# Eight heads' maxima of layer 1 moved among the next element's first scores, value and Gram tiles placed anew

## The chip, the cores and the metric

The kernel runs on one core of a Trainium2 chip. The core has a matrix engine (TensorE, PE in the profile), three engines for elementwise work and reductions (VectorE, DVE; ScalarE, ACT; GpSimd, POOL), and SyncE (SP), which here issues all DMAs. The engines run their own instruction queues in order and meet through semaphores. The metric is the time of one execution on the device in microseconds (us).

## The reference

Two layers of cross attention over 32 elements (B = 32) with 112 queries of 320 channels, 375 context tokens of 512 channels, and 20 heads of 16. Layer 0 attends to 77 text tokens and to the other 298 tokens with separate softmaxes and adds the two. Layer 1 attends to 371 tokens, forms from the same probabilities a mean context vector per head, and lets its cosine with four image tokens add to their scores:

```python
# layer 0
q = heads(x @ Wq.T)
k, v = heads(text @ Wk.T), heads(text @ Wv.T)            # text = ctx[:, :77]
k_ip, v_ip = heads(ip @ Wk_ip.T), heads(ip @ Wv_ip.T)    # ip = ctx[:, 77:]
out = merge(attend(q, k, v)) + merge(attend(q, k_ip, v_ip))
x = out @ Wo.T + bo + x
# layer 1
scores_t = einsum('bhsd,bhtd->bhst', q, k_t) * attn_scale # text = ctx[:, :-4]
probs_t = softmax(scores_t)
text_out = einsum('bhst,bhtd->bhsd', probs_t, v_t)
qsem = l2norm(einsum('bhst,bte->bhse', probs_t, text))
fused = einsum('bhsd,bhnd->bhsn', q, k_ip) * attn_scale + 0.5 * qsem @ l2norm(ip).T
ip_out = (softmax(fused) * side) @ v_ip
x = (text_out + ip_out) @ W_out + b_out + x
```

## The kernel before

All weights stay on the chip. `stage_order` writes out one list of stages (L57 on), and each engine's function walks this same list and does its own part of each stage. So the order of the list is the order of each engine's queue. `o.share(buffer, slots, ...)` notes who may overwrite a buffer when: the next user of a slot waits until the last reader of the one before has signalled.

PSUM has ST (three banks), PN (two banks, PV and NS) and three single banks R. ST and PN have one slot each.

An element b goes through these parts:

- **Keys, queries, values, Gram tiles** (`ahead`): matmuls on the context, split in high and low halves so that three products give full precision. A key tile (`k`) has 12 matmuls, then ScalarE copies the high part, VectorE subtracts it (`rem`) and, in every other tile, casts the middle part; GpSimd makes the low part, SyncE writes all to HBM, from where `k_stack` and `q_stack` load them as Ks and Qs. A value tile (`v_mm`, `v`) and a Gram tile (`g`) have 12 matmuls and are copied by ScalarE, Gram tiles also by VectorE. `split` makes high and low halves of the context of element b + 2: four copies on ScalarE, four subtractions on GpSimd. It needs the last Gram tile of element b.
- **Maxima** (`s_max`): scores of two or three heads with queries in the partitions, 375 columns a head. A step of three heads ("wide") goes to ST, one of two to PN. VectorE reads the maxima to m0 or m1, in layer 1 also the four image scores to `sip`. When all 20 heads are read, `m_T` transposes the maxima on TensorE, ScalarE copies them, GpSimd splits them in three (`m_split`, `mrem` and `ms`), and SyncE writes them as extra rows of Qs, by six DMAs in layer 0 and three in layer 1. The scores need these rows.
- **Scores, exponentials, products with values** (`scores`, `pv0_set`, `pv1`, `y`): groups of four heads, keys in the partitions. Scores go to ST; ScalarE takes the exponential out of ST.
- **Finish** (`pvT`, `o_T`, `o_mm`, `x1_T`, and `ns_T`, `fuse`, `ip_softmax`, `ip_T`, `ip_mm` in layer 1): transposes, output projection and the image part.

The parts of three elements overlap. The order of the list around the change, in one turn of the loop over b: scores of layer 0 of element b with key tiles and queries of b + 1 in between; scores of layer 1 of b - 1; maxima of layer 0 of b + 1, then maxima of layer 1 of b. Among the 16 maxima steps `between` (L413 on) places the finish of b - 1 (`last`), and after steps 2, 4, 6, 8, 11, 12, 14 and 16 one value or Gram tile (`pieces`): layer 1 values 0 to 2 and Gram tiles 0 to 2 of b in turn, at last values 1 and 2 of layer 0 of b + 1. The last of them stands between the last maxima step and the first scores. Right behind the first scores comes `m_T` of layer 1.

Of the kernel before, what the change touches and what calls it, by code (L numbers as in the profile page):

```python
# [1 line left out]

# [13 lines left out]
PV_SETS = ((0, 1, 2), (3, 4))  # L16
SETS_FROM = 2
EPS2 = 1e-24
QROWS = [(0, 3), (3 * D, 2), (5 * D, 1)]
# [11 lines left out]
class Order:  # L31
# [3 lines left out]
    def __init__(self):  # L35
        self.stages, self.nth, self.many = [], {}, {}
        self.ring, self.slot, self.freed = {}, {}, {}

    def add(self, kind, *key):
# [4 lines left out]
    def at(self, kind, *key):  # L44
        return self.nth[kind, key]
# [15 lines left out]
def stage_order():  # L61
# [87 lines left out]

    def maxima(b, l, between):  # L150
        for h in range(0, H, 5):
            for h0, wide in ((h, True), (h + 3, False)):
                o.add("s_max", b, l, h0, wide)
                if wide:
                    o.share("ST", 1, ("s_max", b, l, h0), "s_max_read", o.at("s_max", b, l, h0, wide))
                else:
                    for part in ("PV", "NS"):
                        o.share(part, 1, ("s_max", b, l, h0), "s_max_read", o.at("s_max", b, l, h0, wide))
                between()
        return m_rows(b, l)  # L160

    def m_rows(b, l):
        yield
        o.add("m_T", b, l)
        in_bank(("m_T", b, l), "m_hi", o.at("m_T", b, l))
        yield
        o.add("m_split", b, l)
# [84 lines left out]
    def finish1(b):  # L252
# [22 lines left out]
        o.add("out", b)  # L275

    def take(pieces, n):
        for _ in range(n):
            next(pieces, None)
# [56 lines left out]

    rows0 = maxima(0, 0, among)
    flush()
# [5 lines left out]
    for b in range(B + 1):  # L344
# [3 lines left out]
        first, last = iter(()), iter(())  # L348

        def among0(g):  # L350
            take(rows1, 1)
            if not b and g == 2:
                o.add("k_stack", 1, 0, 0)
            if not b and g == 3:
                o.add("ctx", 2)
            take(pieces, 1 if b + 1 < B and (b or g < 4) else 0)
            if g < 2:
                flush()
# [54 lines left out]
        def between():  # L413
            count[0] += 1
            if count[0] > 9:
                take(rows0, 1)
            if count[0] in (1, 2, 3, 5, 7, 9, 10):
                take(last, 1)
            if count[0] in (2, 4, 6, 8, 11, 12, 14, 16):
                take(pieces, 1)  # L420
            if not b and count[0] > 9:
                warm("R", (4, 0, 2, 3, 2, 3, 3)[count[0] - 10])
            if b + 1 == B:
                warm("R", 2)
        if b + 1 < B:
            rows0 = maxima(b + 1, 0, between)
            take(rows0, 1)
        if b + 1 == B:
            take(pieces, 4)
        if b < B:  # L430
            rows1 = maxima(b, 1, between)
            take(rows1, 1)
# [34 lines left out]
def xattn_two_layers(nc, a, out):  # L467
# [3 lines left out]
    with ctx:  # L471
# [198 lines left out]
        def tensor(e):  # L670
            w = Waiter(e)
            for kind, key in o.stages:
# [119 lines left out]
                elif kind == "s_max":  # L792
                    b, l, h0, wide = key
                    n, to = (3, ST) if wide else (2, PN)
                    w.wait_ge(d_kr[l][0 if h0 + n <= HALVES[0][1] else 1], 96 * (b + 1))
# [11 lines left out]
                elif kind == "m_T":  # L807
                    b, l = key
                    n = 2 * H if l == 0 else H
                    free(w, "R", ("m_T", b, l))  # L810
                    w.wait_ge(s_max_read, 8 * at("m_T", b, l))
                    e.transpose(R[slot["R", ("m_T", b, l)]][0:n, 0:S], (m0, m1)[l][:], ident[0:S, 0:S]).then_inc(m_T, 1)
# [161 lines left out]
        def vector(e):  # L974
# [8 lines left out]
            for kind, key in o.stages:  # L983
# [77 lines left out]
                elif kind == "s_max":  # L1061
                    b, l, h0, wide = key
                    n, to = (3, ST) if wide else (2, PN)
                    w.wait_ge(s_max_mm, at("s_max", *key))
# [619 lines left out]
```

## Time and profile before

| | us |
|---|---|
| median of 3 runs | 2555.74 |
| lowest and highest | 2554.03, 2556.6 |
| span of the profiled execution | 2557.0 |
| TensorE busy (matmuls) | 2466.0 (96%) |
| VectorE busy | 1634.3 (64%) |
| ScalarE busy | 1226.5 (48%) |
| GpSimd busy | 768.3 (30%) |
| mean granted clock of TensorE | 0.994 |

The profiled execution is one more run. Its span is 1.3 us above the median of the others. Busy time of TensorE counts matmuls from start to end, and they overlap, so a wait shows best as the distance from one start to the next. Behind a row of the timeline, "[0.56 <-DVE m L1069]" means that the engine stood idle for 0.56 us until that instruction of VectorE had ended.

### The profile page before, as it was taken

To read this page: it belongs to the slowest core of one execution; us is meant where nothing else is said; L and a number is where in the kernel's file an instruction comes from. 1 tells how busy PE (TensorE), PEld (TensorE's weight loads), DVE (VectorE), ACT (ScalarE), POOL (GpSimd) and SP (SyncE) were. 2 spreads that over 40 slices of the span, in tenths; PEclk is the share of its full clock that TensorE was granted. 3 is DMA by queue.
4 is the path that set the end of the run, shared out by engine and by line. 5 is a ranking of instruction groups with operands and counts; after the bars stand their busy time and mean duration, and the time that the engine had idled before them with its cause. 6 is when DMAs were issued, how large, how long until landed. Compare 5 with 4: busy or idle time off the path is not lost.

```text
span 2557.0 us, 64247 instructions
## 1 busy us (share of the span) xinstructions
PE 2466.0 (96%) x26500; PEld 2147.6 (84%) x26500; DVE 1634.3 (64%) x3217; ACT 1226.5 (48%) x2251; POOL 768.3 (30%) x998
## 2 busy tenths in 40 slices
PE   7899999999999999999999999999999999999998
PEld 7788888888888888888888888888888888888877
DVE  4365667656667666677655677656676656676655
ACT  3355444455444555444554444554444554444543
POOL 3123233232233332333232232332332332332322
PEclk9999999999999999999999999999999999999999
DMA  8765556664456755467655466645566644566620
GB/s 213 135 104 81 93 88 96 104 107 79 88 87 99 117 84 88 85 94 111 103 82 87 84 107 100 109 75 89 97 93 105 93 84 88 88 97 102 94 28 18
DMA packets 373418, 241.47 MB, mean 94 GB/s; under 512 B 133675, under 2 KB 366971, under 8 KB 373116
## 3 DMA queue, kind: packets, MB, share of 16 engines
q1 hardware_dynamic: 373126, 237.36, 56.6%
q8 instruction: 210, 3.44, 0.7%
q14 instruction: 82, 0.67, 0.1%
HBM read 171.35 MB, written 64.59 MB: 92 GB/s over the span
## 4 chain that ended last, share of the span: by engine, by line
PE 76%; DVE 17%; SPq 2%; DMA 2%; issue 2%; ACT 1%; POOL 0%; DVEq 0%; POOLq 0%; ACTq 0%
PE ST L821 7%; DVE w L981 5%; PE R L887 5%; PE PN L860 5%; PE R L763 5%; PE R L708 4%; PE R L776 4%; PE R L777 4%; DVE m L1069 4%; PE R L709 4%; PE PN L905 3%; PE R L945 3%; PE R L779 3%; PE R L711 3%; DVE w L978 2%; PE R L890 2%
## 5 line engine op out<-in xcount | busy, mean ns | idle before, releaser
L1445 POOL TENSOR_TENSOR w<-w 128x448 f32<-128x448 f32 (+1 forms) x256 | 330.8, 1292 | 381.2 <-DVE w L978 362.9
L981 DVE SCALAR_TENSOR_TENSOR w<-p,pr 128x1344 f32<-128x1344 f32 x160 | 296.7, 1854 | 164.1 <-ACT pr L1331 151.5
L1303 ACT ACTIVATE p<-ST 128x1344 f32<-128x1344 f32 x260 | 335.5, 1290 | 102.0 <-PE ST L824 97.0
L887 PE MATMUL R<-pr,Gh 128*128 128x448 f32 (+1 forms) x960 | 366.1, 381 | 0.0
L978 DVE TENSOR_TENSOR rem<-R,kst 128x298 f32<-128x298 f32 (+2 forms) x180 | 89.5, 497 | 425.4 <-ACT kst L1186 425.4
L978 DVE TENSOR_TENSOR w<-R,w 128x448 f32<-128x448 f32 (+1 forms) x480 | 281.7, 620 | 68.5 <-PE R L892 57.8
L1379 POOL TENSOR_TENSOR kst<-rem,kst 128x298 bf16<-128x298 f32 (+2 forms) x180 | 147.9, 822 | 531.5 <-ACT kst L1186 290.9
L776 PE MATMUL R<-wvh,ch 128*128 128x320 f32 (+3 forms) x896 | 302.2, 337 | 0.0
L777 PE MATMUL R<-wvh,cl 128*128 128x320 f32 (+3 forms) x896 | 276.7, 309 | 0.0
L821 PE MATMUL ST<-Qs,Ks 100*128 100x112 bf16 (+1 forms) x3520 | 229.3, 214 | 8.6 <-ACT p L1303 3.5
L821 PEld LDWEIGHTS ST<-Qs,Ks 100*128 100x128 bf16 (+1 forms) x3520 | 188.1, 98 | 47.2 <-issue 14.3
L708 PE MATMUL R<-ch,wkh 128*128 128x298 f32 (+1 forms) x636 | 215.2, 338 | 2.1 <-POOL cl L1379 2.1
L1186 ACT ACTIVATE pvt<-PN 128x112 f32<-128x112 f32 (+2 forms) x260 | 88.7, 341 | 247.7 <-PE PN L909 192.3
L779 PE MATMUL R<-wvl,ch 128*128 128x320 f32 (+3 forms) x672 | 207.4, 309 | 0.0
L1331 ACT ACTIVATE pr<-ST 128x1344 fp32r<-128x1344 f32 x160 | 205.1, 1282 | 0.0
L709 PE MATMUL R<-cl,wkh 128*128 128x298 f32 (+1 forms) x636 | 199.8, 314 | 0.0
L887 PEld LDWEIGHTS R<-pr,Gh 128*128 128x128 f32 (+1 forms) x960 | 175.7, 183 | 22.6 <-issue 6.2
L1073 DVE TENSOR_REDUCE m<-ST 112x3 f32<-112x1113 f32 x128 | 168.0, 1312 | 13.1 <-PE ST L805 13.1
L890 PE MATMUL R<-pr,Gl 128*115 128x448 f32 (+1 forms) x480 | 176.3, 367 | 0.0
L892 PE MATMUL R<-pr,Gl 128*128 128x448 f32 (+1 forms) x480 | 175.6, 366 | 0.0
L1186 ACT ACTIVATE V<-R 128x320 f32<-128x320 f32 (+3 forms) x161 | 67.9, 436 | 211.4 <-PE R L780 211.4
L776 PEld LDWEIGHTS R<-wvh,ch 128*128 128x128 f32 (+3 forms) x896 | 161.0, 180 | 8.0 <-issue 0.5
(221 smaller groups left out, 5956.7 us busy)
## 6 DMA issues: line engine op xcount, KB each, us to landing
Ks<-k_split SPq DMA_DIRECT2D x384, 140.6 KB, 5.8
Ks<-k_split SPq DMA_DIRECT2D x384, 93.8 KB, 7.8
w<-in_ctxT SPq DMA_DIRECT2D x31, 750.0 KB, 9.7
k_split<-kst SPq DMA_DIRECT2D x64, 281.2 KB, 3.6
k_split<-kst SPq DMA_DIRECT2D x64, 223.5 KB, 2.8
Qs<-q_split SPq DMA_DIRECT2D x64, 210.0 KB, 8.2
q_split<-qst SPq DMA_DIRECT2D x128, 84.0 KB, 2.4
Qs<-q_split SPq DMA_DIRECT2D x64, 140.0 KB, 8.4
```

The source lines that it names most:

```text
L708: e.matmul(r[:, 0:t1 - t0], wh[:, k, c0:c0 + 128], h[:, k, t0:t1], start=k == 0, stop=False)
L709: e.matmul(r[:, 0:t1 - t0], wh[:, k, c0:c0 + 128], lo[:, k, t0:t1], start=False, stop=False)
L776: e.matmul(r[0:n, 0:C], h[:, k, :], wh[:, k, :], start=k == 0, stop=False)
L777: e.matmul(r[0:n, 0:C], lo[:, k, :], wh[:, k, :], start=False, stop=False)
L779: e.matmul(r[0:n, 0:C], h[:, k, :], wl[:, k, :], start=False, stop=False)
L821: e.matmul(ST[:, u, S * h:S * h + S], Ks[l][0:m, GH * g + h, 128 * u:128 * u + 128], Qs[l][0:m, GH * g + h, :], start=True, stop=True)
L887: e.matmul(r[0:nj, 0:QW], Gh[0:ROWS[u], q:q + nj], x[0:ROWS[u], QW * u:QW * u + QW], start=u == 0, stop=False)
L890: e.matmul(r[0:nj, 0:QW], Gl[0:ROWS[u], q:q + nj], x[0:ROWS[u], QW * u:QW * u + QW], start=False, stop=False)
L978: return e.tensor_tensor(to, x, y, op)
L981: return e.scalar_tensor_tensor(out=to, in0=x, scalar=s, in1=y, op0=op0, op1=op1)
L1303: e.activation(to.rearrange("p (u q) -> p u q", u=3), st, ACT.Exp).then_inc(p_whole, 1)
L1445: e.tensor_tensor(first, first, w2[n % 2][0:ROWS[j], QW * j:QW * j + QW], ALU.add).then_inc(ns_added, 1)
```

## The change

Elements for which `defers(b)` holds (b = 1 to 30) do only the first 12 heads of layer 1's maxima in their old place: steps of 3, 2, 3, 2 and 2 heads. The other eight heads follow in four steps of two, all in PN, after the first scores of layer 0 of the next element, after its first key tile, after its second scores and after its queries. `m_T` of layer 1 moves from behind the first scores to behind the third, `m_split` behind the first products with values. Among the maxima that stay, the value and Gram tiles come after steps 1, 2, 4, 5, 7, 8, 10 and 12, so that the last step of two heads (in ST) stands right in front of the first scores. `split` moves with the last Gram tile.

```diff
+ALL_STEPS = [(h + d, n, d == 0) for h in range(0, H, 5) for d, n in ((0, 3), (3, 2))]
+NOW_STEPS = [(0, 3, True), (3, 2, False), (5, 3, True), (8, 2, False), (10, 2, True)]
+LATE_STEPS = [(h, 2, False) for h in range(12, H, 2)]
...
-    def maxima(b, l, between):
-        for h in range(0, H, 5):
-            for h0, wide in ((h, True), (h + 3, False)):
-                o.add("s_max", b, l, h0, wide)
...
+    def max_step(b, l, h0, n, wide):
+        key = (b, l, h0, n, wide)
+        o.add("s_max", *key)
+        for part in ("ST",) if wide else ("PV", "NS"):
+            o.share(part, 1, ("s_max", b, l, h0), "s_max_read", o.at("s_max", *key))
+
+    def maxima(b, l, steps, between):
+        for step in steps:
+            max_step(b, l, *step)
+            between()
         return m_rows(b, l)
...
+    def defers(b):
+
+        return SETS_FROM <= b + 1 < B
...
+        late = iter(LATE_STEPS if b and b < B and defers(b - 1) else ())
+
+        def late_step():
+            for step in islice(late, 1):
+                max_step(b - 1, 1, *step)
+
         def among0(g):
-            take(rows1, 1)
+            if b < B and defers(b - 1):
+                late_step()
+                take(rows1, 1 if g > 1 else 0)
+            else:
+                take(rows1, 1)
...
             take(pieces, 1 if b + 1 < B and (b or g < 4) else 0)
+            late_step()
...
-            if count[0] in (2, 4, 6, 8, 11, 12, 14, 16):
+            if count[0] in ((1, 2, 4, 5, 7, 8, 10, 12) if defers(b) else (2, 4, 6, 8, 11, 12, 14, 16)):
                 take(pieces, 1)
...
-            rows1 = maxima(b, 1, between)
+            rows1 = maxima(b, 1, NOW_STEPS if defers(b) else ALL_STEPS, between)
...
-                    w.wait_ge(s_max_read, 8 * at("m_T", b, l))
+                    w.wait_ge(s_max_read, o.max_steps[b, l])
```

VectorE, from the last maxima steps of layer 1 of element 9 to the queries of element 11. Before (L1073 and L1074 read a maxima step, `rem0` is the key tile's remainder, `qrem` and `qst` are the queries'):

```order
L1073 TENSOR_REDUCE m1<-ST 112x3
L1074 COPY sip1<-ST 112x12
L1073 TENSOR_REDUCE m1<-PN 112x2
L1074 COPY sip1<-PN 112x8
L978 TENSOR_TENSOR rem0<-R1,kst0 128x298
L981 SCALAR_TENSOR_TENSOR qrem<-R2,qst 128x336
L1060 CAST qst<-qrem 128x3x112
```

Now (L1094 and L1095 read a maxima step):

```order
L1094 TENSOR_REDUCE m1<-ST 112x2
L1095 COPY sip1<-ST 112x8
L1094 TENSOR_REDUCE m1<-PN 112x2
L1095 COPY sip1<-PN 112x8
L999 TENSOR_TENSOR rem0<-R0,kst0 128x298
L1094 TENSOR_REDUCE m1<-PN 112x2
L1095 COPY sip1<-PN 112x8
L1094 TENSOR_REDUCE m1<-PN 112x2
L1095 COPY sip1<-PN 112x8
L1002 SCALAR_TENSOR_TENSOR qrem<-R1,qst 128x336
L1081 CAST qst<-qrem 128x3x112
L1094 TENSOR_REDUCE m1<-PN 112x2
```

The reads of heads 14 to 17 stand behind the key tile's remainder, and that of heads 18 and 19 behind the cast of the queries.

ScalarE, from the last Gram tile of element 10 (`Gh`, `g4`) to the maxima of layer 0 of element 11 (`mrem`, `ms`); `ch0` is the split, `x1T` the transposed o of element 9, `V1` a value tile. Before:

```order
L1186 ACTIVATE Gh<-R1 128x115
L1186 ACTIVATE g4<-R1 128x4
L1186 ACTIVATE x1T<-R2 128x2x112
L1186 ACTIVATE x1T<-R2 64x112
L1186 ACTIVATE mrem<-R0 40x112
L1186 ACTIVATE ms<-R0 40x112
L1186 ACTIVATE V1<-R2 115x20x16
L1186 ACTIVATE Gh<-R0 115x115
L1186 ACTIVATE g4<-R0 115x4
L1186 ACTIVATE ch0<-w2 128x375 x4
```

Now:

```order
L1207 ACTIVATE Gh<-R0 115x115
L1207 ACTIVATE g4<-R0 115x4
L1207 ACTIVATE ch0<-w2 128x375 x4
L1207 ACTIVATE x1T<-R1 128x2x112
L1207 ACTIVATE x1T<-R1 64x112
L1207 ACTIVATE mrem<-R2 40x112
L1207 ACTIVATE ms<-R2 40x112
```

The last Gram tile and the split have moved ahead of x1T and of the maxima's copies.

GpSimd at the same place (`cl0` is the split's low half). Before:

```order
L1450 TENSOR_TENSOR vbd<-vbd,bmask_sb 80x320
L1379 TENSOR_TENSOR mrem<-mrem,ms 40x112
L1434 CAST ms<-mrem 40x112
L1379 TENSOR_TENSOR ms<-mrem,ms 40x112
L1379 TENSOR_TENSOR cl0<-w2,ch0 128x375 x4
L1386 TENSOR_TENSOR g4<-g4,ninv 128x12
```

Now:

```order
L1471 TENSOR_TENSOR vbd<-vbd,bmask_sb 80x320
L1400 TENSOR_TENSOR cl0<-w2,ch0 128x375 x4
L1407 TENSOR_TENSOR g4<-g4,ninv 128x12
L1400 TENSOR_TENSOR mrem<-mrem,ms 40x112
L1455 CAST ms<-mrem 40x112
L1400 TENSOR_TENSOR ms<-mrem,ms 40x112
```

The split of the layer 0 maxima, which stood ahead of the context's low half, stands behind it.

## Rows read from the trace of the kernel before

**Rows 1.** The page, part 1: busy us (share of the span) and instructions of each engine.

```profile
PE 2466.0 (96%) x26500; PEld 2147.6 (84%) x26500; DVE 1634.3 (64%) x3217; ACT 1226.5 (48%) x2251; POOL 768.3 (30%) x998
```

**Rows 2.** Stretches: us, busy us (instructions) by engine, PEclk, DMA share, GB/s.

```profile
880.68:893.38 12.70, 11.71 (x74) 9.97 (x74) 12.03 (x33) 4.95 (x11) 0.79 (x1) 1.00 0.75 158
893.38:905.87 12.49, 12.23 (x80) 10.56 (x78) 10.66 (x20) 4.17 (x16) 4.78 (x8) 1.00 0.11 29
905.87:911.66 5.79, 5.79 (x69) 5.52 (x68) 0.84 (x4) 4.71 (x9) 1.58 (x4) 1.00 0.02 3
```

**Rows 3.** Timeline of TensorE, the maxima of one element: start us, us, engine, line, what.

```profile
888.51 0.37 PE L803 MATMUL PN<-Ks,Qs 96*112 96x375 bf16 x1 [0.56 <-DVE m L1069]
...
897.01 0.44 PE L776 MATMUL R<-wvh,ch 128*115 128x320 f32 x1
...
898.90 0.32 PE L803 MATMUL PN<-Ks,Qs 96*112 96x375 bf16 x1
...
899.09 0.41 PE L788 MATMUL R<-ch 128*115 128x256 f32 x1
...
900.65 0.48 PE L803 MATMUL ST<-Ks,Qs 96*112 96x375 bf16 x2
```

**Rows 4.** Timeline of VectorE, the same stretch.

```profile
881.36 0.40 DVE L1068 TENSOR_REDUCE m<-ST 112x3 f32<-112x231 f32 x1
...
882.67 0.17 DVE L978 TENSOR_TENSOR zq<-zs 112x20 f32<-112x20 f32 x1
...
883.04 0.31 DVE L1068 TENSOR_REDUCE m<-PN 112x2 f32<-112x154 f32 x1
...
883.95 0.27 DVE L1155 RECIPROCAL sm<-d 112x20 f32<-112x20 f32 x1
...
899.42 0.93 DVE L1073 TENSOR_REDUCE m<-PN 112x2 f32<-112x742 f32 x1 [0.69 <-PE PN L805]
900.27 0.15 DVE L1074 COPY sip<-PN 112x8 f32<-112x8 f32 x1
```

**Rows 5.** Timeline of ScalarE, the same stretch.

```profile
894.34 0.50 ACT L1186 ACTIVATE x1T<-R 128x224 f32<-128x224 f32 x2 [0.27 <-PE R L937]
...
901.06 1.73 ACT L1186 ACTIVATE ch<-w 128x375 fp32r<-128x375 f32 x4
```

**Rows 6.** Timeline of GpSimd, the same stretch.

```profile
895.24 0.39 POOL L1379 TENSOR_TENSOR mrem<-mrem,ms 40x112 f32<-40x112 f32 x1 [10.72 <-ACT ms L1186]
...
896.04 0.39 POOL L1379 TENSOR_TENSOR ms<-mrem,ms 40x112 bf16<-40x112 f32 x1
901.66 3.57 POOL L1379 TENSOR_TENSOR cl<-w,ch 128x375 fp32r<-128x375 f32 x4 [5.22 <-ACT ch L1186]
905.17 0.21 POOL L1386 TENSOR_TENSOR g<-g,ninv 128x12 f32<-128x12 f32 x1
```

**Rows 7.** Timeline of SyncE's queue there; list of DMA issues (KB, us to landing).

```profile
897.76 4.61 SPq L1582 DMA_DIRECT2D Qs<-ms  x6
...
out<-x SPq DMA_DIRECT2D x32, 140.0 KB, 1.9
```

**Rows 8.** Timeline of all engines, behind the first scores of layer 0.

```profile
908.25 0.72 PE L821 MATMUL ST<-Qs,Ks 102*128 102x112 bf16 x11
...
908.90 0.47 DVE L978 TENSOR_TENSOR rem<-R,kst 128x298 f32<-128x298 f32 x1 [2.71 <-ACT kst L1186]
...
911.08 0.71 PE L821 MATMUL ST<-Qs,Ks 102*128 102x112 bf16 x11
...
912.14 0.50 DVE L1060 CAST qst<-qrem 128x336 bf16<-128x336 f32 x1
```

**Rows 9.** Timeline of TensorE near the start, and one stretch there.

```profile
49.30 0.50 PE L803 MATMUL ST<-Ks,Qs 96*112 96x375 bf16 x2 [0.95 <-DMA Qs<-q_split]
...
51.45 0.75 PE L803 MATMUL ST<-Ks,Qs 96*112 96x375 bf16 x2 [0.72 <-DVE m L1069]
...
51.60:55.00 3.40, 3.40 (x15) 3.06 (x15) 3.01 (x6) 0.00 (x0) 0.00 (x0) 0.50 1.07 293
```

More of the change, by code:

```diff
@@ L1 @@
 from contextlib import ExitStack
+from itertools import islice
 import concourse.bass as bass
@@ L37, in __init__ @@
         self.ring, self.slot, self.freed = {}, {}, {}
+        self.max_steps = {}
     def add(self, kind, *key):
@@ L148, in ahead @@
         yield from tail
-    def maxima(b, l, between):
-        for h in range(0, H, 5):
-            for h0, wide in ((h, True), (h + 3, False)):
-                o.add("s_max", b, l, h0, wide)
[L154 to L159, printed above, removed]
+    def max_step(b, l, h0, n, wide):
[7 more added lines that the diff above has]
+            between()
         return m_rows(b, l)
@@ L163, in m_rows @@
         yield
+        o.max_steps[b, l] = o.many["s_max"]
         o.add("m_T", b, l)
@@ L335, in among @@
             warm("R", n)
-    rows0 = maxima(0, 0, among)
+    rows0 = maxima(0, 0, ALL_STEPS, among)
     flush()
@@ L425, in stage_order @@
         if b + 1 < B:
-            rows0 = maxima(b + 1, 0, between)
+            rows0 = maxima(b + 1, 0, ALL_STEPS, between)
             take(rows0, 1)
@@ L792, in tensor @@
                 elif kind == "s_max":
-                    b, l, h0, wide = key
-                    n, to = (3, ST) if wide else (2, PN)
+                    b, l, h0, n, wide = key
+                    to = ST if wide else PN
                     w.wait_ge(d_kr[l][0 if h0 + n <= HALVES[0][1] else 1], 96 * (b + 1))
@@ L1061, in vector @@
                 elif kind == "s_max":
-                    b, l, h0, wide = key
-                    n, to = (3, ST) if wide else (2, PN)
+                    b, l, h0, n, wide = key
+                    to = ST if wide else PN
                     w.wait_ge(s_max_mm, at("s_max", *key))
```

## The prediction

> **What bounds the kernel now.** Read first the busy times: TensorE is busy 96% of the span, VectorE 64%, ScalarE 48% [rows 1]. The 32 elements follow each other on it with hardly a gap, so where it stands still, nothing makes the time good. So I read TensorE in order of time through one element and note only where it stands still and what it waits for. Second, the stretches of this element that the change touches [rows 2]: the maxima (880.68 to 905.87 us, here in two parts of 12.70 and 12.49 us), where VectorE is busy 12.03 and 10.66 us and so nearly as full as TensorE, and the first scores of layer 0 (905.87 to 911.66 us, 5.79 us), where VectorE is busy 0.84 us. The change carries work of VectorE from the full stretch into the empty one. Third, what stands around the places that it touches: TensorE's gaps [rows 3], the maxima's durations on VectorE [rows 4], the queues of ScalarE, GpSimd and SyncE that the Gram tile's new place moves [rows 5 to 7], and VectorE's order among the scores [rows 8].
>
> What the maxima stretch can give back is small. TensorE waits 0.56 us in one piece for VectorE's read of PN [rows 3]; all its waits of this stretch, taken start to start beyond the matmuls' own pitch, are some 2.3 us an element, 0.4 of them for ScalarE's copy of x1T. That is the ceiling of any gain: 30 x 2.3 = 69 us.
>
> **The change, part by part.** I write times from the start of a stretch, all in us. A maximum step costs TensorE 0.16 a head. It costs VectorE 1.31 for three heads (881.36 to 882.67) and 0.91 for two (883.04 to 883.95) in layer 0; in layer 1 the read of two starts 0.52 after the step's first matmul (898.90, 899.42) and ends with the copy at 1.52 (899.42 to 900.27, and 0.15) [rows 3, 4]. ST and PN have one buffer each, so the next writer waits for that end.
>
> *First twenty heads (layer 0 of the next element).* Six value and Gram tiles stand among them instead of four. The two that come in took 1.89 and 1.56 (897.01 to 898.90, 899.09 to 900.65) [rows 3], so without any other effect the part would go from 12.70 to 16.15. I walked TensorE and VectorE through the new order with the durations of rows 4: the third read on VectorE (and the rest behind it) now stands behind the first Gram tile's low half, which waits for ScalarE, so the step of heads 10 to 12 waits 0.8, the transpose of the image weights 0.4, the step of heads 15 to 17 0.3. It comes to 15.7: a gain of 0.5. Ends: 0 and 1.7 (all waits of this part).
>
> *From the last Gram tile to the scores.* Call the end of the Gram tile G (900.65 before). ScalarE starts the copies of its high half at G+0.20 and the split of the next-but-one context at G+0.41, which takes 1.73 (900.65, 901.06) [rows 3, 5]. Before, the o transposes and their copy to x1T had gone ahead of the split. Now the split stands ahead of them on ScalarE, so x1T, whose two copies take 0.50 [rows 5], is there at G+2.6. TensorE, with one wide step, the transposes, one narrow step and the maxima's transpose in between (1.2), waits 1.4 where it waited 0.4. Its rest takes 6.3: output matmul 1.62, two value tiles 1.77 each, steps of 3, 2 and 2 heads: G+8.9 without further waits.
>
> The second and larger price is on GpSimd and SyncE. The low halves of the split (3.57, from G+1.01) and the scaling of g (ends at G+4.73) stood behind the three instructions that split the layer 0 maxima; now these stand behind them [rows 6]. They take 1.19 (895.24 to 896.43), so they end at G+5.9. Only then does SyncE issue six DMAs of 4.4 KB with the maxima's rows of Qs, 4.61 one after another [rows 7]; the last needs 1.1 more to land if I set it by the 1.9 that a single out DMA takes from issue to landing [rows 7], less its own issue (a sixth of 4.61). They land at G+11.7, and scores of layer 0 wait for them. Before, they were issued from 897.76 and had 8.1 until the scores at 905.87. So scores start at G+11.7, and TensorE stands still for 2.8. Lower bound: if the DMAs were not last, the scores would wait for VectorE's read of the step just ahead of them (the value tile that covered it is now in front of that step): 1.52 + 0.1 - 0.32 = 1.3, scores at G+10.2. Upper: 3.5, if GpSimd is held up by 0.7.
>
> The part took 12.49; less the two tiles (3.45) and eight heads (1.28) it is 7.8; it becomes 11.7: a loss of 4.0. The maxima stretch is then 15.7 + 11.7 = 27.4 instead of 25.2: **+2.2**.
>
> The Trainium skill says (DMA: Bandwidth & Descriptors, Issuing engines are not separate DMA queues) that the sequencer's time to initiate a DMA "is usually small relative to the DMA itself". In the trace it is the larger part for these six [rows 7]. By the page the rows of Qs would land early and the sum would lose this wait; that is rival C.
>
> *Eight heads among the scores.* The four steps bring 1.28 of matmuls and, in VectorE's order, put the reads behind other things. The step of heads 14 and 15 is read behind the key tile's remainder. The key tile ended at 908.25; after ScalarE's copy the remainder starts 0.65 later and takes 0.47; in about half of the elements a cast follows, some 0.3 by my estimate from the queries' larger one of 0.50 [rows 8]. So that read starts 1.05 to 1.4 after the tile and ends 2.0 to 2.4 after it. TensorE has the step itself (0.32) and scores 1 (0.57) to do, then the step of heads 16 and 17 needs PN: it waits 1.2 to 1.5. The step of heads 18 and 19 is read behind the remainder and cast of the queries: queries end at 911.08, the cast ends at 912.64 [rows 8], the read 0.9 later, 2.55 after the queries with latency. TensorE has 0.32 + 0.57 to do, and then stands at the transpose of layer 1's maxima, which now needs that last read: it waits 1.6. Sum: 1.28 + 1.35 + 1.6, **+4.2**. Ends: 2.0 (reads slip in during ScalarE's waits, which the fixed order of VectorE speaks against) and 5. Hidden at no cost: the transposed maxima's way to Qs of layer 1 (it starts some 9 later, and scores of layer 1 come 14 after that), the extra VectorE instructions (two per element in an idle stretch), the earlier value copies.
>
> *Clock.* TensorE's granted clock is full in every stretch of the middle of the run. It fell in the first and last elements, after stretches in which TensorE stood still: 0.95 and 0.72 close together (49.30, 51.45), then the clock 0.50, 1.2 GHz instead of 2.4, for 51.60 to 55.00, where two matmuls took 0.75 instead of 0.50 [rows 9]. The new wait ahead of the scores, 2.8 in one piece, is longer than those two together. I expect a fall at some five of six such places. A fall of 3.4 costs half of it, 1.7, a longer one up to twice that; I take 1.8 a place, between 0 and 3.4.
>
> **Sum.** Elements 1 to 30 have the new maxima stretch: 30 x 2.2 = 66. Twenty-nine full elements have the late heads, 29 x 4.2 = 122, and the last element 1 (no key or query work stands there): 123. Clock 30 x 1.8 = 54. Together 243. Profiled span 2557.0 + 243 = 2800; the median of the runs shown is 1.3 below the span, so 2799.
>
> **Rivals.**
> B, no falls of the clock: the same waits, but none long enough. For it: the waits among the maxima left the clock full [rows 2, 3]. 2557 + 189 - 1 = 2745.
> C, the rows of Qs land in time (SyncE's issue overlaps, or GpSimd gets to the maxima sooner): scores wait 1.3 instead of 2.8, and no fall. 2745 - 30 x 1.5 = 2700.
> D, more falls: the waits of 1.4 and 1.6 among the scores also bring the clock down, or each fall is long: 30 x 3.4 instead of 1.8, and some 0.7 more an element: 2799 + 30 x 2.3 = 2868.
> E, faster: VectorE's nearly empty scores stretch [rows 2] takes the reads at once. It decides at the read of heads 14 and 15: if it ends within 0.9 of its matmuls, TensorE never waits for it, the waits among the maxima go and only the 1.28 of matmuls moves. 30 x 2.3 = 69 less: 2487. Against it stands the order in which VectorE waits for ScalarE first [rows 8], and nothing in it helps the DMAs.
> F, no change: the new waits are taken back later in the element. Against it: TensorE has no slack of this size behind the scores.
>
> **How the numbers follow.** Forecast 0.55; B 0.20; C 0.08; D 0.08; E 0.05; F 0.04. The range goes from between C and B to D's near side: 2715 to 2865, leaving out most of C, half of D, E and F, some 0.2. A measurement of this kernel can tell about 0.2% from no change. Faster by over 0.2%: 0.05; within 0.2%: 0.03; slower: 0.92.
>
> **What would show it.** In the trace of after: the wait of PE at L842 (scores of layer 0) for a DMA into Qs, some 2.7 each, 30 times; PE at L824 (PN) for VectorE's copy of sip, 1.2 to 1.5 right behind scores 1; PE at the maxima's transpose L833, 1.6; PE at the output matmul for ScalarE's x1T, 1.4; the maxima stretch 27.4 instead of 25.2, and 9.9 instead of 5.8 from the first scores to the second key tile; PEclk under 9 in many slices. Wrong would be: PE's waits at L842 for VectorE (then C), PEclk full throughout (then B), or shorter stretches than before (E).

## The result, and the profile after

| | before | after |
|---|---|---|
| median of the runs, us | 2556.17 (4 runs) | 2804.28 (4 runs) |
| lowest and highest | 2554.03, 2558.89 | 2797.96, 2806.97 |
| span of the profiled execution | 2557.0 | 2803.2 |
| mean granted clock of TensorE | 0.994 | 0.971 |

The changed kernel takes 1.0966 times as long (95% interval 1.0953 to 1.098). Forecast were 2799 us, range 2715 to 2865. It is slower, and by the size forecast; what follows asks whether by the causes forecast too.

Part 1 of the page of after answers to [rows 1]; of part 2 the row of the granted clock in 40 slices:

```profile
PE 2528.8 (90%) x26500; PEld 2198.8 (78%) x26500; DVE 1645.3 (59%) x3277; ACT 1234.6 (44%) x2251; POOL 766.0 (27%) x998
...
PEclk9999999999999999999999999999999999999989
```

TensorE has the same 26500 matmuls, and its share has fallen from 96% to 90%. VectorE has 60 instructions and 11 us more, ScalarE 8 us, so no other engine has noticeably more to do. So the time went into TensorE's waits, and 63 us of it into matmuls that took longer. PEclk is an average in tenths over 70 us and hides this: the forecast had it under 9 in many slices, and one slice of 40 shows 8.

TensorE's longest sums of waits in after (engine, what for; us in all, times, longest):

```profile
PE R L833 <- DVE sip L1095: 111.1, 61, 2.2
...
PEld ST L842 <- DMA Qs<-ms: 69.4, 32, 3.5
...
PE ST L842 <- DMA Qs<-ms: 51.6, 26, 3.3
PE PN L824 <- DVE sip L1095: 34.9, 31, 1.4
PE ST L824 <- DVE m L1090: 18.7, 32, 0.9
...
PE ST L842 <- DVE sip L1095: 7.1, 6, 1.2
```

L824 is a maxima step, L833 the transpose `m_T`, L842 the scores. The scores wait for the DMAs into Qs, as forecast, but 26 times, 2 us each, and not 30 times 2.8; six more times they wait for VectorE's last read. PN behind scores 1 is waited for 31 times, 1.1 each. The largest sum was not foreseen in this form: `m_T` waits 61 times, so in both layers; the forecast has it in layer 1 alone.

The same stretches as in [rows 2], of an element of after: first twenty heads, last Gram tile to scores, scores to the second key tile.

```profile
954.51:970.05 15.54, 14.72 (x97) 13.20 (x98) 13.18 (x35) 5.92 (x15) 0.79 (x1) 1.00 0.76 142
970.05:981.96 11.91, 7.85 (x49) 6.38 (x47) 6.29 (x12) 4.04 (x13) 4.70 (x8) 1.00 0.05 14
981.96:992.01 10.05, 8.64 (x74) 7.99 (x74) 4.15 (x9) 4.16 (x6) 0.75 (x1) 0.83 0.16 44
```

In the second stretch TensorE is busy 7.85 of 11.91 us, where before it was busy 12.23 of 12.49. This is where to look. TensorE in order of time, one step of the first stretch (heads 10 to 12 of layer 0), then the second stretch and what is behind it:

```profile
962.58 0.50 PE L824 MATMUL ST<-Ks,Qs 96*112 96x375 bf16 x2 [0.56 <-DVE m L1090]
...
970.05 0.48 PE L824 MATMUL ST<-Ks,Qs 96*112 96x375 bf16 x2
...
973.25 0.26 PE L833 MATMUL R<-ident_sb,m 112*40 112x112 f32 x1 [1.94 <-DVE sip L1095]
...
979.36 0.32 PE L824 MATMUL ST<-Ks,Qs 96*112 96x375 bf16 x1
...
981.96 1.21 PE L842 MATMUL ST<-Qs,Ks 102*128 102x112 bf16 x11 [2.12 <-DMA Qs<-ms]
...
988.16 0.37 PE L824 MATMUL PN<-Ks,Qs 96*112 96x375 bf16 x1 [1.01 <-DVE sip L1095]
...
993.32 0.26 PE L833 MATMUL R<-ident_sb,m 112*20 112x112 f32 x1 [1.71 <-DVE sip L1095]
```

GpSimd and SyncE in the second stretch (answering to [rows 6] and [rows 7]):

```profile
971.06 3.52 POOL L1400 TENSOR_TENSOR cl<-w,ch 128x375 fp32r<-128x375 f32 x4 [10.31 <-ACT ch L1207]
...
975.52 0.39 POOL L1400 TENSOR_TENSOR ms<-mrem,ms 40x112 bf16<-40x112 f32 x1
```

```profile
975.77 0.33 SPq L1614 DMA_DIRECT2D out<-x  x1
976.15 4.61 SPq L1603 DMA_DIRECT2D Qs<-ms  x6
```

With G = 970.05, the maxima are split at G+5.9, and the six DMAs are issued from G+6.1 for 4.61 us. The scores start at G+11.9. The forecast had G+5.9, 4.61 and G+11.7. But SyncE does not start on `ms` alone: an output DMA stands ahead of the six, and it was issued at G+5.7. That row is what the experiments turn on.

VectorE behind the scores, answering to [rows 8]:

```profile
986.73 0.47 DVE L999 TENSOR_TENSOR rem<-R,kst 128x298 f32<-128x298 f32 x1 [1.80 <-ACT kst L1207]
987.11 0.92 DVE L1094 TENSOR_REDUCE m<-PN 112x2 f32<-112x742 f32 x1
...
991.76 0.50 DVE L1081 CAST qst<-qrem 128x336 bf16<-128x336 f32 x1
992.18 0.92 DVE L1094 TENSOR_REDUCE m<-PN 112x2 f32<-112x742 f32 x1
```

The reads of the late heads stand behind the remainder and the cast, and TensorE waits for them at 988.16 and 993.32.

The table gives the parts of an element in us, from the starts of TensorE's stages in the traces (mean of 22 elements in the middle of the run). In brackets stands the lowest, where no fall of the clock is in it.

| kernel | scores 0 to 2nd key tile | on to the maxima | first 20 heads | G to scores 0 | element |
|---|---|---|---|---|---|
| before | 5.72 | 46.28 | 12.7 | 12.5 | 77.2 |
| after | 10.87 (9.83) | 46.34 | 15.54 | 12.73 (11.89) | 85.5 |
| e1_mt | 11.50 | 46.61 | 15.54 | 11.81 (11.68) | 85.5 |
| e2_tiles | 7.71 (6.19) | 46.29 | 15.54 | 13.09 | 82.6 |
| e3_late | 10.35 (10.10) | 47.04 | 23.9 with the next | | 81.3 |
| e4_split | 10.78 | 46.45 | 15.56 | 12.65 (11.89) | 85.4 |
| e5_both | 11.04 | 46.67 | 15.55 | 10.26 (10.17) | 83.5 |
| e6_three | 10.00 | 46.46 | 15.56 | 12.24 (10.98) | 84.3 |
| e7_mended | 10.01 (9.85) | 46.54 | 15.53 | 9.31 | 81.4 |
| e8_spaced | 6.32 (6.15) | 51.51 | 15.54 | 11.03 (10.27) | 84.4 |
| e9_best | 6.31 | 46.76 | 15.55 | 8.52 | 77.1 |
| e10_warm | 10.01 (9.84) | 46.90 | 15.55 | 11.82 (11.77) | 84.3 |
| e11_cover | 10.01 (9.85) | 46.98 | 15.56 | 12.58 (11.89) | 85.1 |
| e12_pairs | 6.30 | 46.64 | 13.93 | 9.11 | 76.0 |

(Before has two tiles fewer among its first 20 heads and two more behind G. Of its late heads, e8 has four ahead of the second key tile and e9 and e12 have six, instead of eight; these three have two heads more behind G. In e12 the last step of the first 20 heads stands behind G too. Without a fall the first column of after, e7 and e10 is 9.85 or 10.20, element by element, and 10.01 in the mean.) Ratios below are against runs of before on the same chip.

### The profile page after: what moved, and what is told of

Its sections match the earlier page's. It is cut to its first block, busy times and chain, and to the rows that moved or that the text cites. A ratio compares the mean times of both kernels' runs of the same rounds, so it can differ in the third digit from the quotient of the medians.

```text
span 2803.2 us, 64277 instructions
## 1 busy us (share of the span) xinstructions
PE 2528.8 (90%) x26500; PEld 2198.8 (78%) x26500; DVE 1645.3 (59%) x3277; ACT 1234.6 (44%) x2251; POOL 766.0 (27%) x998
## 4 chain that ended last, share of the span: by engine, by line
PE 64%; DVE 22%; SPq 5%; issue 3%; DMA 3%; ACT 3%; POOL 0%; DVEq 0%; POOLq 0%; ACTq 0%
PE ST L842 5%; DVE w L1002 5%; PE R L908 4%; PE PN L881 4%; PE R L784 4%; PE R L729 4%; DVE m L1094 4%; DVE m L1090 4%; PE R L730 4%; SPq L1603 3%; PE R L966 3%; PE PN L926 3%; PE R L797 3%; PE R L798 3%; PE R L732 3%
## 5 line engine op out<-in xcount | busy, mean ns | idle before, releaser
L797 PE MATMUL R<-wvh,ch 128*128 128x320 f32 (+3 forms) x896 | 318.7, 356 | 0.0
L842 PE MATMUL ST<-Qs,Ks 100*128 100x112 bf16 (+1 forms) x3520 | 236.8, 218 | 62.3 <-DMA Qs<-ms 51.6
L842 PEld LDWEIGHTS ST<-Qs,Ks 100*128 100x128 bf16 (+1 forms) x3520 | 198.8, 100 | 109.2 <-DMA Qs<-ms 69.4
L798 PE MATMUL R<-wvh,cl 128*128 128x320 f32 (+3 forms) x896 | 282.7, 315 | 0.0
L729 PE MATMUL R<-ch,wkh 128*128 128x298 f32 (+1 forms) x636 | 226.0, 355 | 3.2 <-POOL cl L1400 3.2
L1094 DVE TENSOR_REDUCE m<-PN 112x2 f32<-112x742 f32 x188 | 173.8, 924 | 91.9 <-PE PN L826 91.9
L1400 POOL TENSOR_TENSOR cl<-w,ch 128x375 fp32r<-128x375 f32 x124 | 109.3, 914 | 412.3 <-ACT ch L1207 412.3
L730 PE MATMUL R<-cl,wkh 128*128 128x298 f32 (+1 forms) x636 | 206.6, 325 | 0.0
L797 PEld LDWEIGHTS R<-wvh,ch 128*128 128x128 f32 (+3 forms) x896 | 168.4, 188 | 14.2 <-issue 4.7
```

The lines of the kernel that those rows point to most:

```text
L729: e.matmul(r[:, 0:t1 - t0], wh[:, k, c0:c0 + 128], h[:, k, t0:t1], start=k == 0, stop=False)
L730: e.matmul(r[:, 0:t1 - t0], wh[:, k, c0:c0 + 128], lo[:, k, t0:t1], start=False, stop=False)
L797: e.matmul(r[0:n, 0:C], h[:, k, :], wh[:, k, :], start=k == 0, stop=False)
L798: e.matmul(r[0:n, 0:C], lo[:, k, :], wh[:, k, :], start=False, stop=False)
L842: e.matmul(ST[:, u, S * h:S * h + S], Ks[l][0:m, GH * g + h, 128 * u:128 * u + 128], Qs[l][0:m, GH * g + h, :], start=True, stop=True)
L1094: e.reduce_max(m1[:, h0:h0 + n], to[0:S, 0:n, 0:TEXT1], X)
```

## The unforeseen wait at the maxima's transpose (e1)

In after, `m_T` of layer 0 waits for `o.max_steps`, the count of all reads noted so far, and the count is taken when `m_T` is placed, two steps of layer 1 later. Edit (e1_mt): the count is taken before the `yield` for layer 0.

```diff
     def m_rows(b, l):
+        if l == 0 or not defers(b):
+            o.max_steps[b, l] = o.many["s_max"]
         yield
-        o.max_steps[b, l] = o.many["s_max"]
+        if l == 1 and defers(b):
+            o.max_steps[b, l] = o.many["s_max"]
```

> The changed kernel, but the transpose of layer 0's maxima waits only for layer 0's reads (in the changed kernel its count is taken late and holds two steps of layer 1, so TensorE waits some 2.0 us for them). Theory: the scores behind it wait for the DMAs of Qs anyway, so the 2.0 us were hidden: scores still start some 11.7 us after the last Gram tile, 2795 to 2815 us. Rival: that wait is part of the loss; then the kernel gets 30 x 0.6 us or more faster, 2785 us or below.

Measured: 2791.82 us, ratio 1.0916 (1.0885 to 1.0947), 12 us less than after; the profiled executions differ by 2 (spans 2801.0 and 2803.2). The waits of e1:

```profile
PE ST L845 <- DMA Qs<-ms: 82.5, 32, 4.5
PE R L836 <- DVE sip L1098: 50.7, 30, 1.7
PE R L969 <- ACT x1T L1210: 37.9, 30, 1.3
```

The time lies between the two expectations. 60 us of waits at `m_T` are gone, and hardly any time. 38 of them come back one matmul later as the wait for x1T that the forecast had (1.3 each, forecast 1.4), and 31 at the scores, which wait 2.6 each (forecast 2.8). So the unforeseen wait stands in series with two forecast ones and mostly covers them. That is why the sum came out although this wait was missed.

## Which chain the scores wait for (e4, e5, e6, e11)

*Split behind the maxima* (e4_split): the split of the next context is placed behind the maxima's own instructions.

```diff
-                if t == 2 and b + 2 < B:
+                if t == 2 and b + 2 < B and not defers(b):
                     o.add("split", b + 2)
...
+            if count[0] == 11 and defers(b) and b + 2 < B:
+                o.add("split", b + 2)
```

> The changed kernel with one stage moved: the split of the next context behind the split of layer 0's maxima. Theory: GpSimd reaches the maxima at once, the DMAs of Qs are in time, scores wait only for VectorE's read of the last step: 12.7 us after the Gram tile become some 11, and falls of the clock ahead of the scores vanish: 2745 us (2725 to 2765). Rival: the rows of Qs are not what scores wait for: 2795 to 2810 us.

Measured: 2801.95 us, ratio 1.0953 (1.0936 to 1.097). The theory failed; nothing moved. An element of e4 with G = 882.53 shows why, on GpSimd and on SyncE:

```profile
886.50 0.39 POOL L1402 TENSOR_TENSOR mrem<-mrem,ms 40x112 f32<-40x112 f32 x1 [3.16 <-ACT ms L1209]
...
887.31 0.39 POOL L1402 TENSOR_TENSOR ms<-mrem,ms 40x112 bf16<-40x112 f32 x1
```

```profile
888.25 0.33 SPq L1616 DMA_DIRECT2D out<-x  x1
888.62 4.63 SPq L1605 DMA_DIRECT2D Qs<-ms  x6
```

GpSimd is done at G+5.2, 0.7 earlier than in after, but the output DMA is issued at G+5.7 as before. It needs x, x needs the output matmul, and that stands behind `m_T` and its wait. Two chains end within 0.2 us of each other, so mending either one alone gives nothing. This asks for both edits at once.

*Both* (e5_both): the edits of e1 and e4.

> The changed kernel with two edits at once: the transpose of layer 0's maxima waits only for layer 0's reads (as in e1_mt), and the split of the next context stands behind the instructions that split layer 0's maxima (as in e4_split). Theory: two chains end together some 6 us after the last Gram tile, the split of the maxima on GpSimd and the output DMA that stands ahead of the six DMAs on SyncE and waits for x_added; each edit alone leaves the other chain, so each alone gave nearly nothing. Together the six DMAs are issued from some 4.5 us after the Gram tile and land at 10.3, the scores of layer 0 wait 0.5 to 1 instead of 1.9: 12.7 becomes about 10.5, less some falls of the clock, 2735 (2715 to 2760). Rival: the scores wait for something else than these rows; then it stays at the 2792 of e1_mt.

Measured: 2742.31 us, ratio 1.0725 (1.0706 to 1.0745): 62 us less than after, where the two edits alone gave 12 and 2. SyncE in an element with G = 866.59:

```profile
870.60 0.33 SPq L1619 DMA_DIRECT2D out<-x  x1
870.98 4.61 SPq L1608 DMA_DIRECT2D Qs<-ms  x6
```

The six DMAs go from G+4.4, and the scores start at G+10.2. They still wait 2.1 us: now it is the issue alone that they wait for.

*Three DMAs instead of six* (e6_three), the same bytes, the rows of Qs and of the ones facing them in another order:

```diff
-                    for c in range(2 if l == 0 else 1):
-                        for u in range(3):
-                            r0 = 96 + 3 * c + u
-                            e.dma_start(Qs[l][r0:r0 + 1, :, :], ms[H * c:H * c + H, u, :]).then_inc(d_m[l], 16)
+                    n = 2 if l == 0 else 1
+                    for u in range(3):
+                        e.dma_start(Qs[l][96 + n * u:96 + n * u + n, :, :], ms[0:H * n, u, :]).then_inc(d_m[l], 16)
```

> The changed kernel with three DMAs of layer 0's maxima into Qs instead of six (each takes both halves of the element's columns; the rows of Qs and of the ones that face them are ordered accordingly; the same bytes). Theory: it is SyncE's issue of about 0.77 each that the scores of layer 0 wait for, so the last lands 2.3 earlier, and the scores then wait for VectorE's read of the last step, some 10.9 us after the last Gram tile instead of 12.7: 30 x 1.8 = 54 less, about 2745 (2735 to 2765). Rival: the issue time goes with the bytes and not with the number of DMAs; then three take the same 4.6 and the time stays at 2804.

Measured: 2767.09 us, ratio 1.082 (1.0804 to 1.0837). SyncE and, 3.5 us later, the scores:

```profile
880.03 2.06 SPq L1602 DMA_DIRECT2D Qs<-ms  x3
```

```profile
885.55 0.65 PE L842 MATMUL ST<-Qs,Ks 102*128 102x112 bf16 x10 [1.19 <-DVE sip L1095]
```

Three DMAs of twice the bytes are issued in 2.06 us (0.69 each) instead of 4.61 (0.77 each). The issue time goes with their number. The scores no longer wait for Qs but 1.2 for the last read, and without a fall of the clock they start at G+10.98 (expected 10.9). The gain is 37 us and not 54, since a fall of the clock now sits at the output matmul in most elements (mean G+12.24). The rival, that the bytes set the issue time, is out.

*The last value tile behind the last step* (e11_cover), positions `(1, 2, 4, 5, 7, 8, 10, 13)` instead of `(..., 10, 12)`:

> The changed kernel with one edit: the last value tile stands between the last maxima step and the scores of layer 0, instead of ahead of that step. Theory: the scores wait for the rows of Qs and not for the last read, so covering that read gives nothing: 2795 to 2810. Rival: the last read is what they wait for; then up to 1.4 less an element, 2762.

Measured: 2793.94 us, ratio 1.093 (1.0906 to 1.0954). This is 1 us below the range expected: the tile fills the wait at the scores, and the wait moves in front of the step. The scores start at G+11.89 at the earliest, to the hundredth as in after, so the rival (the last read is what they wait for) is out. The 10 us less go with 34 falls of the clock instead of 44, none of them in the first column.

## Either half of the change alone (e2, e3)

*New tile places, no late heads* (e2_tiles), with the count for `m_T` taken early: `late = iter(())`, `maxima(b, 1, ALL_STEPS, between)`, `m_T` of layer 1 behind the first scores as before.

> Only the new places of the value and Gram tiles (all 20 heads of layer 1 in their old place, transpose of layer 0's maxima waits for layer 0's reads alone). Theory: the last steps stand without tiles between them, TensorE waits for VectorE's reads, and scores for the rows of Qs: scores start some 12.8 us after the last Gram tile, 30 x 3.2 us on 2557, 2650 us, up to 2690 if the clock falls. Rival: the tiles' places are harmless and the eight heads are the whole loss: 2550 to 2570 us.

*Late heads, old tile places* (e3_late), count as in e1: `count[0] in (2, 4, 6, 8, 11, 12, 14, 16)`.

> Only the eight late heads (tiles in their old places, transpose of layer 0's maxima as in the run before). Theory: the late reads behind the key remainder and the query cast cost 4.2 us an element among the scores, of which 1.3 are matmuls taken out of the maxima; no wait for Qs, no fall of the clock: 2557 + 29 x 2.9 = 2642 us. Rival: these waits replace others later on, 2560 to 2590 us.

Measured: e2 2711.67 us, ratio 1.0609 (1.0579 to 1.064); e3 2672.18 us, ratio 1.0445 (1.0426 to 1.0465). Both halves lose, 155 and 115 us, and both lose more than I had expected. In e2 the maxima stretch is 28.6 us instead of 25.2: the last steps follow each other with fewer tiles between, and the list of waits has 34.1 us for ST at the steps and 25.8 at the scores, both for VectorE's reads; the clock falls 31 times. In e3 the stretch is 23.9, so the late heads do give back 1.3 there, but the way to the second key tile grows by 4.4 without a fall, and 18 falls cost some 16 us more than the 7 of before.

## What the clock costs (e10)

Falls of the granted clock in after, as stretches with the columns of [rows 2]. The first begins at the scores of the element above, the others at the output matmul and at the scores of the next one:

```profile
981.91:985.32 3.41, 3.36 (x21) 3.27 (x22) 1.00 (x2) 1.29 (x1) 0.00 (x0) 0.50 0.21 58
1057.00:1060.41 3.41, 3.41 (x9) 2.10 (x9) 0.08 (x1) 0.84 (x3) 2.26 (x6) 0.50 0.02 5
1067.24:1070.65 3.41, 3.41 (x23) 3.31 (x21) 1.00 (x2) 1.29 (x1) 0.00 (x0) 0.50 0.19 53
```

The clock record of after holds 44 stretches at 0.50 (1.2 GHz), 164.5 us in all, nearly all 3.4 long; that of before holds 7, 32.8 us. In e10_warm matmuls whose results nobody uses stand in the two waits:

```diff
         if b < B:
+            if b and defers(b - 1):
+                warm("R", 8)
             (groups0 if b < SETS_FROM else sets0)(b, among0)
...
+        if l == 0 and b and defers(b - 1):
+            warm("R", 8)
         o.add("m_T", b, l)
```

> The changed kernel with extra matmuls, whose results nobody uses, ahead of layer 0's first scores and ahead of the transpose of layer 0's maxima, where TensorE otherwise stands for about 2 us each; nothing waits for less than before. Theory: these two stops are what brings the granted clock down to 0.5 some 43 times for 3.4 us, each fall costing 1.7; filled, they cost their own length as before but no fall: 2804 - 43 x 1.7 + some 5 to 20 for matmuls that outlast the wait = 2735 to 2755. Rival: the falls have another cause or cost nothing; then it stays at 2804 or above.

Measured: 2761.85 us, ratio 1.0811 (1.0791 to 1.0832), span 2758.1; 2735 to 2755 was expected. More work on the busiest engine makes the kernel 42 us faster. 13 falls are left (50.7 us), and PE keeps its waits behind the scores; the eight falls in the middle of the run all come right behind `m_T` of layer 1. So 31 falls fewer, 114 us at half the clock, give back 45 us of span and not 57. Those at the scores cost 1.5 each (the median of after in the first column is 11.35, the lowest 9.83). Those at the output matmul have two prices. In 24 elements in the middle of the run ten have a fall that begins 4.2 us or more behind G, and their scores start at G+12.5 to 12.9 instead of 11.9: 0.7 to 1.0, since a wait for Qs follows that the slower matmuls shorten. Seven have one that begins 3.0 to 3.7 behind G, at the output matmul itself, and start at G+13.2 or later: 1.3 and more. I take it that there the output DMA and the six behind it come later too; no run tests this.

## Towards a version that gains (e7, e8, e9, e12)

*All of it mended but the late heads* (e7_mended): e1, e4, e6 and e11 together.

> The changed kernel with all that concerns the stretch ahead of layer 0's scores mended: the transpose of the maxima waits for layer 0's reads alone, the split stands behind the maxima's, three DMAs instead of six, and the last value tile stands between the last step and the scores. The late heads among the scores stay as they are. Theory: the scores start some 8 to 9 us after the last Gram tile instead of 12.7, so that the maxima stretch is about 24.5 instead of 28.3 and shorter than the 25.2 of the kernel before; what is left is the late heads' waits of 1.3 and 1.9 and the falls of the clock behind them: 2804 - 30 x 3.8 - 45 of clock = about 2645 (2630 to 2680). Rival: the stretch is bound by VectorE's reads rather than by the rows of Qs; then 2700 or more.

Measured: 2682.76 us, ratio 1.0489 (1.0471 to 1.0506). The stretch from G to the scores is 9.3 us with no wait for Qs, and the maxima stretch 24.8, shorter than the 25.2 of before. What is left of the loss, 124 us, stands among the scores: 4.3 us an element. The time is 3 us above the range expected, because a wait of 1.3 remains in front of the step of heads 10 and 11.

*Late steps apart* (e8_spaced): six late heads, steps behind scores 0, behind the queries and behind the third key tile, `m_T` of layer 1 a group of scores and a tile behind the last.

> As e7_mended without the tile's later place, but only six late heads, and these spaced: one step behind scores 0, one behind the queries, one behind the cast-free key tile, and the transpose of layer 1's maxima two tiles after the last of them, so that no step follows within 2 us of another. Theory: the loss among the scores was the distance of the steps from their reads, not the steps: the two waits of 1.3 and 1.9 go, the clock does not fall there, and the scores stretch grows by the matmuls alone (0.96) while the maxima stretch loses as much and some waits: 2540 to 2570, within 0.5% of before (2557). Rival: VectorE's order, remainder and cast first, delays the reads wherever they stand; then 60 to 100 us more than before.

Measured: 2766.01 us, ratio 1.0812 (1.0796 to 1.0829). The time missed by 200 us, the mechanism among the scores of layer 0 did not: the first column is 6.32, which is before plus the steps' own matmuls. But `m_T` stands 16 us behind the scores, and at the scores of layer 1 this appeared:

```profile
908.92 0.71 PE L851 MATMUL ST<-Qs,Ks 100*128 100x112 bf16 x11 [3.01 <-DMA Qs<-ms]
```

```profile
904.90 0.39 POOL L1409 TENSOR_TENSOR ms<-mrem,ms 20x112 bf16<-20x112 f32 x1
```

```profile
900.79 3.63 SPq L1569 DMA_DIRECT2D k_split<-kst  x3
905.32 2.40 SPq L1611 DMA_DIRECT2D Qs<-ms  x3
```

From `m_T` (901.07) to the scores it is 7.9 us: GpSimd has the maxima split only at 905.29, since a key tile's low part stands ahead of them, and the three DMAs take 2.40. The trace holds 50 falls of the clock, 29 of them behind this wait. (In the edit the last value tile does stand behind the last step, as in e7, other than the expectation says.) The prediction had called this way free, and in after it is, because `m_T` comes 5 us earlier.

*Steps ahead of a tile* (e9_best): against e8 the late steps stand ahead of the first key tile, the queries and the second key tile, `m_T` right behind that, and the other steps in pairs:

```diff
+                if g < 3:
+                    late_step()
...
             take(pieces, 1 if b + 1 < B and (b or g < 4) else 0)
+            if b < B and defers(b - 1) and g == 2:
+                take(rows1, 2)
...
+            if count[0] in ((1, 2, 4, 5, 7, 8, 12, 14) if defers(b) else (2, 4, 6, 8, 11, 12, 14, 16)):
```

> Against e8_spaced the late steps stand ahead of a tile instead of behind one: six late heads, one step each ahead of the first key tile, the queries and the second key tile among the scores of layer 0, the transpose of layer 1's maxima right behind that key tile; among the maxima the steps stand in pairs with a tile between the pairs (two steps, output matmul, two steps, value tile, two steps, value tile). Theory: a read on VectorE then stands ahead of the remainder that waits for ScalarE, and TensorE has a tile to do meanwhile, so that none of the late steps is waited for; layer 1's rows of Qs are under way 8 us earlier than in e8_spaced and its wait of 3.3 goes; the maxima stretch is 24.8 - 1.3 + 0.3 = 23.8 and the scores stretch 0.96 longer than before: 77.16 - 0.4 an element, 2546 (2535 to 2565). Rival: what was gained is lost to the clock or to reads that still come late: 2600 or more.

Measured: 2548.46 us, ratio 0.997 (0.9959 to 0.998). VectorE's read of heads 16 and 17 still stands behind the remainder, as in after:

```profile
902.36 0.47 DVE L1005 TENSOR_TENSOR rem<-R,kst 128x298 f32<-128x298 f32 x1 [1.11 <-ACT kst L1213]
902.84 0.93 DVE L1100 TENSOR_REDUCE m<-PN 112x2 f32<-112x742 f32 x1
```

My reason (the read ahead of the remainder) holds for one of the three. But all three have a tile of TensorE, 1.8 to 2.0 us, between themselves and the next user of PN, and in e9 no late step is waited for in the middle of the run.

*Tiles in pairs too* (e12_pairs): the same rule for the first twenty heads, the first two Gram tiles each with a value tile behind it.

```diff
-                take(pieces, 1)
+                take(pieces, {1: 1, 3: 2, 5: 2, 7: 1, 12: 1, 14: 1}.get(count[0], 0) if defers(b) else int(count[0] in (2, 4, 6, 8, 11, 12, 14, 16)))
```

> Against e9_best one more move, among the maxima of layer 0: the value tiles and Gram tiles stand two together (Gram tile, then value tile), so that no step stands right behind a Gram tile, whose low half VectorE computes when ScalarE is done, with the steps' reads queued behind it. Theory: the two waits ahead of the steps of heads 10 and 13 there (some 0.9 and 0.4 an element in e9_best) go, and some of it comes back at the steps that now stand closer together: 0.5 to 1.0 less an element, 2520 to 2535. Rival: VectorE has 8.7 us of reads in this part however they are placed, and the steps that now follow each other wait as much: 2540 to 2560; with more than 2560 the clock or a wait for ScalarE came in instead.

Measured: 2513.43 us (2512.05 to 2514.82), ratio 0.9831 (0.9817 to 0.9844): 1.7% faster than before. It was 7 us better than expected: the element is 1.1 us shorter than in e9, and little came back (17 us in all, the first wait below). The stretches of [rows 2] in an element of e12, and its longest waits that recur in every element:

```profile
942.36:956.25 13.89, 13.89 (x95) 13.09 (x95) 11.72 (x33) 5.95 (x15) 0.79 (x1) 1.00 0.66 130
956.25:965.36 9.11, 8.46 (x52) 6.78 (x51) 8.55 (x18) 3.59 (x12) 4.71 (x8) 1.00 0.15 39
```

```profile
PE PN L829 <- DVE m L1095: 17.0, 32, 0.6
PE R L900 <- DVE w L1004: 15.0, 31, 0.6
```

## Why the prediction was right

- **What bounds the kernel** was read rightly: TensorE has no slack, each wait is added to the end. Spans grew by 246.2. By the table 30 x 2.2 = 66 of them are the maxima stretch, 29 x 4.3 = 124 the late heads and some 51 the falls of the clock; 5 have no place in the parts that I walked. Without the clock 195 were measured and 189 forecast.
- **First twenty heads**: 15.7 forecast, 15.54 measured. Of the three waits the first, forecast at 0.8, shows 0.56 of idle time at 962.58.
- **G to the scores**: G+11.7 forecast, G+11.89 measured where the clock stayed full, and so 27.4 for the maxima stretch, as forecast. The waits inside were not as forecast: 2.1 at `m_T` and 2.3 at the scores (start to start), instead of 1.4 at the output matmul and 2.8. The step that failed is the reading of the wait count: `o.max_steps` is taken after the `yield`, which the kernel shows (the lines are in e1's edit) and I took for the same place. e1 shows that it cost at most 12 us, since a DMA chain sets the end. That the missed wait covered two forecast ones, and so left the time as forecast, is luck.
- **The DMA chain**: right in its times, incomplete in its cause. I had GpSimd's order alone; e4 and e5 show the output DMA ahead on SyncE as a second chain of the same length. Undoing only what I had named gave 2 us.
- **Rival C** fell. The Trainium skill (DMA: Bandwidth & Descriptors, Issuing engines are not separate DMA queues) calls the time to initiate a DMA usually small relative to the DMA; here six take 4.61 us, and the scores follow 1.2 after the last issue. One of them takes 0.77 to issue, which is not small beside these 1.2, and what the scores wait for is six in a row. Halving their number (e6) removed the wait, as the rows and not this sentence had it.
- **Late heads**: 4.2 forecast, 4.3 measured (10.01 in e7 and e10, whose falls lie elsewhere, against 5.72). The wait at PN is 1.2 or 1.5, start to start, as forecast, that at `m_T` 1.9 instead of 1.6.
- **Clock**: 30 places of 1.8, 54 us, forecast. Measured were 37 falls more than before. By the table they cost 0.86 an element among the scores (10.87 against 10.01) and 0.84 behind G (12.73 against 11.89), by my estimate 30 x 1.7 = 51 us; e10 took 31 of them away and gave back 45. The size was right by two errors that cancel, which is luck: I had one place an element, and there are two; and I took each fall at its full half, while most of those at the output matmul cost 0.7 to 1.0. Rival B is out by this, and D by its size. But D's mechanism, falls behind the late waits, is real: they come in e3 and e10, once the waits ahead of the scores are gone or filled.
- **Rival E** fell: the read of heads 14 and 15 stands behind the remainder, as forecast. In e9 and e12, with a tile between a step and the next user of its buffer, no late head is waited for, and e12 gets 44 us below before. How much of this the late heads bring is not shown, since no run has the tiles' places, DMAs and split of e12 without late heads.

## What to carry to other kernels

When a step is moved, look for the second chain that ends at the same place. Two chains of equal length hide each other, and an edit to one of them shows little (2 and 12 us alone, 62 together). A step whose result another engine reads belongs ahead of a tile that the first engine can do meanwhile, and not right behind one whose copy the reader must wait for. Where such steps stand matters: eight late heads with the tiles in their old places cost 115 us (e3), and with six of them ahead of tiles the element is as long as before (e9, 77.1 against 77.2 us).

## What the runs showed of the hardware

- A DMA of 4.4 KB took 0.77 us of SyncE to issue, one of 8.8 KB 0.69 (e6): fewer and larger DMAs shorten a tail, even with the same bytes.
- Extra matmuls in two waits of 2 us each made the kernel 42 us faster, since the granted clock fell to 0.50 only 13 times instead of 44 (e10). Nearly every fall lasted 3.4 us. It cost 1.5 us at the scores, where work followed, and at the output matmul 0.7 to 1.0 or 1.3 and more, by where it began (after).
